# Expert biases and parameters gathered from one table, only where a stream's expert changes

## Chip, cores and metric

The kernel runs on one core of a Trainium2 chip. The time is the device time of one launch in microseconds (us); the number given for a kernel is the median of its runs. The profile is of one further execution.

## What is computed

The program is one layer of a graph network, a linear-attention mixer beside it, and a mixture of experts on their sum. The change touches the mixture of experts alone. It has 1250 rows of width D = 512, 16 experts, the best two experts for a row, and a hidden width I = 384 (so the first product makes 768 columns, gate and up interleaved):

```python
def swiglu5(h, alpha, gate_scale, up_shift, gate_clamp_raw, up_clamp_raw):
    gate_clamp = jax.nn.softplus(gate_clamp_raw)
    up_clamp = jax.nn.softplus(up_clamp_raw)
    g = jnp.clip(h[..., ::2], -gate_clamp, gate_clamp)
    u = jnp.clip(h[..., 1::2], -up_clamp, up_clamp)
    return g * jax.nn.sigmoid(g * alpha) * gate_scale * (u + up_shift)
...
gate_probs = jax.nn.softmax(xf @ gate_w + gate_b, -1)
w, idx = jax.lax.top_k(gate_probs, 2)
w = w / jnp.sum(w, axis=-1, keepdims=True)
he = jnp.einsum('nd,edh->enh', xf, expert_w1) + expert_b1[:, None, :]
te = swiglu5(he, a[:, 0], a[:, 1], a[:, 2], a[:, 3], a[:, 4])   # a = expert_act, five numbers an expert
oe = jnp.einsum('enh,ehd->end', te, expert_w2) + expert_b2[:, None, :]
y = jnp.einsum('ne,end->nd', cw, oe)                            # cw: the two weights of each row
return y + z                                                    # z: the same with a shared expert
```

## The kernel before

`moe` (from line 2285) is a program with semaphores written out by hand for five engines. It sorts the 2500 (row, expert) pairs into tiles of 64 rows with one expert each (HALF = 64). There are room and indices for 54 tiles. They are laid out as six streams of nine tiles (STREAMS = 6, TURNS = 9), and a stream is a run of consecutive tiles with a weight buffer of its own (`ew1[s]`, `ew2[s]`). Two streams work side by side: stream 2k on partitions ("lanes") 0 to 63, stream 2k+1 on lanes 64 to 127. So the loop has 27 steps, PAIRS = 27. Step i works on side `i % 3`, that is streams 2(i % 3) and 2(i % 3)+1, at turn `i // 3`. The bias ring has three buffers too (U = 3), so buffer `i % U` belongs to side `i % 3`.

For the inputs of the reference the experts get 71, 5, 1044, 7, 450, 335, 0, 2, 12, 2, 1, 13, 245, 0, 313 and 0 rows, which is 49 filled tiles. Along the streams the expert of the next turn is another one after step 2, 3, 5, 6, 7 and 8 in the even stream alone, after steps 4 and 11 in both, after step 22 in the odd and after step 23 in the even one: 12 changes in the 48 stream turns.

Routing first: POOL scatters the rows into their slots in DRAM with indirect DMAs (line 2478, ten for each of the two choices), while PE computes the shared expert. Then, for each step i:

- PE transposes the slot rows (line 2805), forms the first product (`up_pe`, line 2820, in two pieces of columns), transposes the gated rows (line 2868) and forms the second product (line 2883). The first piece of step i+1 stands ahead of the transposes of step i, its second piece ahead of the second product of step i. The first piece of step i waits for `next_w1_in` of both its streams.
- DVE adds the biases to the first product (`glu_dve`, line 2918, reads `eb1[u]`), clips (2922, 2923) and multiplies (2925, 2928). ACT takes the sigmoid (2944) with the expert's factor. All take their scalars from `eprm[u]`.
- ACT scales the result with the row's weight (line 2963), POOL scatters it to DRAM (line 2993).
- POOL gathers the weights for the next turn of both streams with one indirect DMA for each stream and matrix (`next_weights`, line 2972): those of w1 once `up_mm` of step i is there, those of w2 once `down_mm` is. The index table `weights_of` has an index beyond the bound for every lane but lane 0 where the expert stays the same, so those rows are skipped. A w1 row is 12,288 bytes in a lane, a w2 row 6,144.
- SP's `load_bias(i + 3)` loads the biases of the step three further on as soon as the buffer is free (`glu_made`): for each of the two streams it reads the expert's number from `slot_expert` into a register, then issues one DMA that spreads the expert's 768 biases over 64 lanes (line 2755, 192 KB) and one that spreads its eight parameters (line 2757, 2 KB, from `param_dram`). `load_slots` loads the slot rows, ten steps ahead.

POOL's indirect DMAs run on the software queue (q0 in the profile), SP's on a hardware queue (q1). Both use the same 16 DMA engines. All helper DMAs of SP carry line 114, so they are told apart by their tiles: `m_eb`, `m_eprm`, `rows`.

Of the kernel before, what the change touches and what calls it, by code (L numbers as in the profile page):

```python
# [16 lines left out]
ds = bass.ds  # L17
# [2267 lines left out]
def moe(c, x, w_all, cols_mem, cols, rows, slot_dram, back_dram, out):  # L2285
# [17 lines left out]
    param_dram = nc.dram_tensor("swiglu_params", [EXPERTS + 1, 8], F32)  # L2303
# [16 lines left out]
    first_w2_in = [c.sem(f"e_first_w2_in{s}") for s in range(STREAMS)]  # L2320
    next_w1_in = [c.sem(f"e_next_w1_in{s}") for s in range(STREAMS)]
    next_w2_in = [c.sem(f"e_next_w2_in{s}") for s in range(STREAMS)]
    weights_of_made = c.sem("r_weights_of_made")
# [9 lines left out]
    with ExitStack() as ctx:  # L2333
# [4 lines left out]
        eb1 = ring("m_eb1_", [128, 2 * FFN_I])  # L2338
        eprm = ring("m_eprm", [128, 8])
# [78 lines left out]
        rounds = lambda tile: tile // U + 1  # L2418
# [6 lines left out]
        def route_sp():  # L2425
            sp = c.sp
            load(sp, prm[0:EXPERTS, 0:5], a["L0_ffn_expert_act"]).then_inc(prm_in, 16)
            load(sp, prm[EXPERTS:EXPERTS + 1, 0:5], a["L0_ffn_shared_act"].rearrange("(a n) -> a n", a=1)).then_inc(
                prm_in, 16)
            load(sp, shared_b2[:], a["L0_ffn_shared_b2"].partition_broadcast(P)).then_inc(b2_in, 16)  # L2430
            for n in range(2):
                load(sp, b1[:, n, :], a["L0_ffn_shared_b1"].rearrange("(c p n) -> p n c", p=128, n=2)[:, n, :]).then_inc(
                    b1_in, 16)
            for q in range(SIDE):
                load(sp, b2[q * SQUARE:q * SQUARE + EXPERTS, :], a["L0_ffn_expert_b2"]).then_inc(w2_in, 16)
            load(sp, w2, chunks(a["L0_ffn_shared_w2"])).then_inc(w2_in, 16)
            sp.wait_ge(prm_made, 2)
            load(sp, param_dram[:, :], prm[:]).then_inc(prm_passed, 16)
            sp.wait_ge(prm_passed, 16)
            load(sp, shared_prm[:], param_dram[EXPERTS, :].partition_broadcast(128)).then_inc(prm_passed, 16)  # L2440
# [129 lines left out]
        def slots_dve():  # L2570
# [173 lines left out]
        def load_bias(i):  # L2744
            sp = c.sp
            u = i % U
            if i >= U:
                sp.wait_ge(glu_made, i - U + 1)
            for e, s in enumerate(streams(i)):
                j = tile_of(s, turn(i))  # L2750
# [24 lines left out]
        def experts_sp():  # L2775
# [4 lines left out]
            for i in range(U):  # L2780
                load_bias(i)
# [127 lines left out]
        def glu_dve(i):  # L2909
# [4 lines left out]
            v.wait_ge(bias_in[u], 64 * rounds(i))  # L2914
# [3 lines left out]
            v.tensor_tensor(by_half(h[u]), by_unit(psum[0:128, at:at + 2 * FFN_I]), by_unit(eb1[u][:]), ALU.add).then_inc(  # L2918
# [18 lines left out]
        def sigmoid(i):  # L2937
            s = c.act
            u = i % U
            s.wait_ge(bias_in[u], 64 * rounds(i))  # L2940
# [24 lines left out]
        def experts_pool():  # L2965
# [11 lines left out]
            g.wait_ge(weights_of_made, 1)  # L2977
            for i in range(PAIRS):
# [115 lines left out]
```

## Time and profile before

| | |
|---|---|
| median of 3 runs | 2438.06 us (2435.76 to 2438.35) |
| the profiled execution | 2439.28 us |
| its span, first to last instruction | 2437.3 us |
| mean granted TensorE clock | 0.993 |
| last first-piece matmuls (step 26) start | 2398.94 us |
| expert loop | about 2144 to 2407 us of the span |

The page gives PE busy for 97% of the span. The parts to read are those of the expert loop: the windows of it (busy time of each engine, the granted clock, the share of the 16 DMA engines' time in use, GB/s), the idle time of PE ahead of an instruction and what released it, the DMA queues by window, and POOL's own order of time.

### The profile page before, as it was taken

The page shows a single profiled execution, that of the slowest core. Times are in us where ns is not written, and L with a number is a line of the kernel's source. Part 1 is how long each engine was busy: PE and PEld are TensorE (multiplying, and loading weights), DVE is VectorE, ACT ScalarE, POOL GpSimd, SP SyncE. Part 2 cuts the span into 40 slices and gives each one's busy share as a digit, 9 for nine tenths or more (in the row PEclk, how much of TensorE's full clock was granted, in tenths as well). Part 3 has the DMA queues.
Part 4 walks back from the last instruction along what each step waited for, and adds up shares of the span by engine and source line. Part 5 has one row for each costly group of instructions (what it writes and reads, how often), then busy time and mean ns, then how long its engine had stood idle before and what let it go on. Part 6 is the DMA issues. An engine that isn't in the chain of part 4 may idle for free. (4 is left out here: it accounts for less than half of the span.)

```text
span 2437.3 us, 27998 instructions
## 1 busy us (share of the span) xinstructions
PE 2368.2 (97%) x9345; PEld 1402.0 (58%) x9345; DVE 1413.3 (58%) x2941; ACT 962.6 (39%) x1663; POOL 896.7 (37%) x1247
## 2 busy tenths in 40 slices
PE   8999999999999999999999999999999999988998
PEld 4565655545676556577556567666567664533443
DVE  7897671432776653677654477655377565633345
ACT  5885643221665211466221266321166422212221
POOL 2005202030565430365341165351065534434564
PEclk9999999999999999999999999999999999999999
DMA  5401101330566310366210266410066611679637
GB/s 166 138 18 32 44 13 52 93 102 18 134 156 156 124 57 18 90 152 156 80 42 22 57 159 156 124 42 22 18 150 161 165 41 48 219 251 322 215 89 235
DMA packets 138367, 264.31 MB, mean 108 GB/s; under 512 B 53038, under 2 KB 54814, under 8 KB 135884
## 3 DMA queue, kind: packets, MB, share of 16 engines
q1 hardware_dynamic: 93214, 159.89, 22.7%
q0 software_dynamic: 43664, 100.31, 15.4%
q10 hardware_dynamic: 1346, 2.33, 0.3%
q8 instruction: 76, 1.25, 0.2%
q14 instruction: 67, 0.55, 0.1%
HBM read 212.90 MB, written 31.93 MB: 100 GB/s over the span
## 5 line engine op out<-in xcount | busy, mean ns | idle before, releaser
L114 POOL DMA_DIRECT2D cols<-w x720 | 353.7, 499 | 592.7 <-DVE w L808 576.9
L691 PE MATMUL psum<-cols,rows 128*128 128x256 f32 (+1 forms) x1600 | 371.1, 380 | 7.2 <-DMA cols<-w 7.2
L677 PE MATMUL psum<-g_k_cols,g_q_cols 128*125 128x512 f32 (+1 forms) x960 | 362.0, 514 | 2.5 <-DVE g_row_max L794 2.5
L871 ACT ACTIVATE g_prob<-g_prob,g_row_max 125x1250 f32<-125x1250 f32 x160 | 214.0, 1338 | 307.9 <-DVE g_row_max L794 306.2
L691 PEld LDWEIGHTS psum<-cols,rows 128*128 128x128 f32 (+1 forms) x1600 | 303.8, 190 | 47.5 <-DMA cols<-w 8.6
L794 DVE CUSTOM_DVE_ANT_0 g_prob<-psum,ln_count 125x1250 f32<-125x1250 f32 x160 | 233.6, 1460 | 142.8 <-PE psum L677 142.8
L677 PEld LDWEIGHTS psum<-g_k_cols,g_q_cols 128*125 128x125 f32 x960 | 179.8, 188 | 173.2 <-issue 161.5
L808 DVE STREAM_TRANSPOSE w<-g_prob 128x1280 f32<-128x1280 f32 x160 | 241.2, 1508 | 11.2 <-ACT g_prob L877 11.2
L877 ACT ACTIVATE g_prob<-g_prob,g_row_max 125x1250 f32<-125x1250 f32 x160 | 214.1, 1338 | 58.3 <-DVE g_row_max L784 58.3
L2820 PE MATMUL psum<-m_ew,m_x_cols 128*64 128x256 f32 (+1 forms) x576 | 155.0, 499 | 16.9 <-DMA cols<-in_L_ffn_expert_w,m_weights_of 7.5
L704 PE MATMUL psum<-g_wo,g_q_cols 128*125 128x512 f32 x320 | 143.7, 593 | 1.8 <-ACT g_q_cols L883 1.8
L747 PE MATMUL psum<-w,g_k_cols 128*125 128x512 f32 x320 | 143.6, 592 | 0.0
L661 PE MATMUL psum<-w,cols 128*128 128x512 f32 (+1 forms) x320 | 139.3, 592 | 0.0
L2918 DVE TENSOR_TENSOR m_work<-psum,m_eb 128x768 f32<-128x768 f32 x27 | 40.9, 1514 | 150.3 <-PE psum L2820 129.8
L379 PE MATMUL psum<-cols,w 128*128 128x375 f32 (+1 forms) x416 | 115.3, 426 | 0.0
L661 PEld LDWEIGHTS psum<-w,cols 128*128 128x128 f32 (+1 forms) x320 | 60.0, 187 | 71.7 <-issue 71.5
L379 PE MATMUL psum<-rows,w 128*128 128x375 f32 (+1 forms) x368 | 101.2, 426 | 0.0
L2820 PEld LDWEIGHTS psum<-m_ew,m_x_cols 128*64 128x64 f32 x576 | 58.8, 139 | 72.9 <-issue 64.6
L333 POOL TENSOR_TENSOR rows<-cols 128x750 f32<-128x750 f32 (+1 forms) x16 | 20.7, 1293 | 211.6 <-ACT cols L515 211.6
L2972 POOL DMA_INDIRECT m_ew<-in_L_ffn_expert_w,m_weights_of x64 | 64.9, 1015 | 87.6 <-PE psum L2883 58.4
L1667 DVE TENSOR_SCALAR p_shared<-iota,p_edge_sum 125x250 f16<-125x250 f16 x334 | 95.3, 286 | 0.0
L429 DVE TENSOR_TENSOR g_k_cols<-g_k_cols,psum 128x375 f32<-128x375 f32 (+1 forms) x32 | 15.4, 481 | 136.6 <-PE psum L379 136.6
(392 smaller groups left out, 3936.5 us busy)
## 6 DMA issues: line engine op xcount, KB each, us to landing
cols<-w POOLq DMA_DIRECT2D x720, 80.0 KB, 3.3
cols<-w SPq DMA_DIRECT2D x560, 80.0 KB
m_eb<-in_L_ffn_expert_b SPq DMA_DIRECT2D x54, 192.0 KB
w<-in_L_gnn_m_w SPq DMA_DIRECT2D x8, 1024.0 KB
slot_rows<-p_kf SPq DMA_DIRECT2D x1, 7128.0 KB, 32.7
rows<-slot_rows SPq DMA_DIRECT2D x54, 132.0 KB, 5.2
m_ew<-in_L_ffn_expert_w SPq DMA_DIRECT2D x4, 1536.0 KB, 14.5
slot_outputs<-slot_rows SPq DMA_DIRECT2D x1, 5000.0 KB
```

What stands on the lines that cost most here:

```text
L114: return eng.dma_start(out, in_, allow_slow_non_contiguous=True)
L379: ins = pe.matmul(c.bank(SEVEN_BANKS[p][u], width), left, right, start=(k == 0 and p in (1, 5, 6, 7)), stop=(k == 1), skip_group_check=True)
L661: ins = pe.matmul(c.bank(V_BANKS[t], D, r), y_cols[:, k, t * 128:t * 128 + r], w[2][:, k, :], start=(k == 0), stop=(k == KC - 1))
L677: ins = pe.matmul(psum[0:P, at:at + width], q_cols[:, h, t * P:(t + 1) * P], k_cols[:, h, start:start + width], start=True, stop=True)
L691: ins = pe.matmul(c.bank(6 + g % 2, 256).rearrange("p (u a i) -> p u a i", u=2, a=SIDE), rows[0:r, j, h * 128:(h + 1) * 128], turned_keys[ ...
L704: ins = pe.matmul(c.bank(t % 2, D, P), q_cols[:, k, t * P:(t + 1) * P], wo[:, k, :], start=(k == 0), stop=(k == KC - 1))
L747: ins = pe.matmul(c.bank(t % 2, D, P), k_cols[:, k, t * P:(t + 1) * P], w[2][:, k, :], start=(k == 0), stop=(k == KC - 1))
L794: v.tensor_tensor_reduce(prob[0:P, u, 0:N], psum[0:P, at:at + N], ln_count[:, t, :], -SCORE_SCALE, -NOT_AN_EDGE / 10, ALU.add, ALU.min, ro ...
L808: v.transpose(square[s][:, :, u, :].rearrange("p b (j i) -> p b j i", i=SQUARE), prob_squares[u]).then_inc(squared, 1)
L871: s.activation(prob[0:P, u, 0:N], prob[0:P, u, 0:N], ACT.Exp, bias=row_max[:, u, 0:1], scale=-1.0, accum_out=row_max[:, u, 2:3]).then_inc( ...
L877: s.activation(prob[0:P, u, 0:N], prob[0:P, u, 0:N], ACT.Identity, scale=row_max[:, u, 3:4]).then_inc(prob_made, 1)
L2820: ins = pe.matmul(psum[lanes(e), at:at + cn], x_cols[u][:, k, lanes(e)], ew1[s][:, k, c0:c0 + cn], start=(k == 0), stop=(k == KC - 1))
```

## The change

One DRAM table, `unit_params`, gets a row of 776 numbers for each expert: 768 biases and 8 parameters. SP fills it during routing with two DMAs. The first three steps' buffers are loaded from it by SP as before, with one DMA for each stream instead of two. All later ones are gathered by POOL with one indirect DMA for each step (128 lanes, index table `bias_of`) into the side's buffer, between the gathers of w1 and of w2, after a wait for `glu_made`. `bias_of` skips as `weights_of` does: where a stream's expert stays, its lanes (but lane 0) are skipped and the buffer keeps what it has. DVE makes `bias_of` with three more small operations behind `weights_of`. `eprm` is now a view of the last eight columns of `eb1`.

```diff
@@ routing
             sp.wait_ge(prm_made, 2)
-            load(sp, param_dram[:, :], prm[:]).then_inc(prm_passed, 16)
+            load(sp, unit_dram[:, 0:2 * FFN_I], a["L0_ffn_expert_b1"]).then_inc(units_passed, 16)
+            load(sp, unit_dram[:, 2 * FFN_I:UNIT_ROW], prm[0:EXPERTS]).then_inc(units_passed, 16)
+            load(sp, param_dram[:, :], prm[EXPERTS:EXPERTS + 1]).then_inc(prm_passed, 16)
             sp.wait_ge(prm_passed, 16)
-            load(sp, shared_prm[:], param_dram[EXPERTS, :].partition_broadcast(128)).then_inc(prm_passed, 16)
+            load(sp, shared_prm[:], param_dram[0, :].partition_broadcast(128)).then_inc(prm_passed, 16)
...
             v.tensor_copy(weights_of[:], weights_f[:]).then_inc(weights_of_made, 1)
+            v.scalar_tensor_tensor(expert_f[:, 1:], same[:, 1:], lane_of[:, 1:2], expert_f[:, 1:], ALU.mult,
+                                   ALU.add).then_inc(step, 1)
+            n += 1
+            v.wait_ge(step, n)
+            for e in range(2):
+                v.tensor_copy(bias_of[lanes(e)].rearrange("p (q s) -> p q s", s=SIDES),
+                              expert_f[lanes(e)].rearrange("p (s e q) -> p e q s", e=2, q=TURNS)[:, e]).then_inc(
+                                  weights_of_made, 1)
@@ SP
-        def load_bias(i):
+        def load_first_bias(i):
...
-                load(sp, eb1[u][lanes(e), :], a["L0_ffn_expert_b1"][ds(of, 1), :].rearrange(
-                    "l o -> (l o)").partition_broadcast(HALF)).then_inc(bias_in[u], 16)
-                load(sp, eprm[u][lanes(e), :], param_dram[ds(of, 1), :].rearrange(
-                    "l o -> (l o)").partition_broadcast(HALF)).then_inc(bias_in[u], 16)
+                load(sp, eb1[i][lanes(e), :], unit_dram[ds(of, 1), :].rearrange("l o -> (l o)").partition_broadcast(
+                    HALF)).then_inc(bias_in[i], 16)
...
             for i in range(PAIRS):
-                if i + U < PAIRS:
-                    load_bias(i + U)
                 if i + R < PAIRS:
                     load_slots(i + R)
@@ DVE and ACT
-            v.wait_ge(bias_in[u], 64 * rounds(i))
+            v.wait_ge(*((next_bias_in[u], 16 * turn(i)) if turn(i) else (bias_in[u], 32)))
...
@@ POOL
                     next_weights(i, ew1, w1_rows, next_w1_in)
+                    g.wait_ge(glu_made, i + 1)
+                    g.indirect_dma_start(
+                        out=eb1[side(i)][:], out_offset=None, in_=unit_dram[:, :],
+                        in_offset=bass.IndirectOffsetOnAxis(ap=bias_of[:, i + SIDES:i + SIDES + 1], axis=0),
+                        bounds_check=EXPERTS - 1, oob_is_err=False).then_inc(next_bias_in[side(i)], 16)
                     g.wait_ge(down_mm, i + 1)
                     next_weights(i, ew2, w2_rows, next_w2_in)
```

## Rows read from the trace of the kernel before

**Rows 1.** The page's first part: busy us, share of the span, instructions.
```profile
PE 2368.2 (97%) x9345; PEld 1402.0 (58%) x9345; DVE 1413.3 (58%) x2941; ACT 962.6 (39%) x1663; POOL 896.7 (37%) x1247
```
**Rows 2.** Windows: stretch, its us, engines' busy us, PE clock, DMA share, GB/s.
```profile
2084.00:2090.00 6.00, 6.00 (x16) 2.77 (x15) 5.39 (x18) 1.85 (x3) 3.96 (x5) 1.00 0.96 390
...
2189.00:2264.00 75.00, 62.19 (x343) 26.81 (x341) 25.29 (x35) 15.48 (x28) 36.94 (x48) 0.95 1.02 317
2280.00:2302.00 22.00, 20.16 (x116) 8.39 (x114) 10.10 (x14) 5.58 (x10) 12.98 (x17) 1.00 0.91 304
2302.00:2400.00 98.00, 98.00 (x567) 42.53 (x569) 44.48 (x79) 24.36 (x45) 58.42 (x75) 1.00 0.43 134
```
**Rows 3.** Chain that ended last: start us, us, what; steps 2 and 5, a wait.
```profile
2167.88 3.65 PE psum L2820 x16
...
2194.50 3.43 PE psum L2820 x16
2197.93 0.48 PE psum L2868 x3
2198.41 0.44 PE psum L2805 x4
2198.84 1.88 PE psum L2820 x16
2200.72 2.60 PE psum L2883 x12
...
2249.80 14.39 DMA m_ew<-in_L_ffn_expert_w,m_weights_of
```
**Rows 4.** PE in order of time: start, us, ..., [idle before it, releaser].
```profile
2204.90 3.65 PE L2820 MATMUL psum<-m_ew,m_x_cols 128*64 128x512 f32 x16 [1.60 <-DMA m_ew<-in_L_ffn_expert_w,m_weights_of]
2220.01 1.08 PE L2820 MATMUL psum<-m_ew,m_x_cols 128*64 128x512 f32 x1 [6.09 <-DMA cols<-in_L_ffn_expert_w,m_weights_of]
2233.97 0.61 PE L2820 MATMUL psum<-w,m_x_cols 128*64 128x512 f32 x1 [2.15 <-DMA m_ew<-in_L_ffn_expert_w,m_weights_of]
2253.52 0.61 PE L2820 MATMUL psum<-m_ew,m_x_cols 128*64 128x512 f32 x1 [1.39 <-DMA cols<-in_L_ffn_expert_w,m_weights_of]
2264.44 0.61 PE L2820 MATMUL psum<-w,m_x_cols 128*64 128x512 f32 x1 [1.90 <-DMA m_ew<-in_L_ffn_expert_w,m_weights_of]
2301.92 3.65 PE L2820 MATMUL psum<-m_ew,m_x_cols 128*64 128x512 f32 x16 [1.10 <-DMA m_ew<-in_L_ffn_expert_w,m_weights_of]
```
**Rows 5.** DMA queues (packets, MB, share of 16 engines) and issues, 2189 to 2264.
```profile
q0 software_dynamic: 4371, 19.13, 80.0%
q1 hardware_dynamic: 3263, 4.55, 21.7%
...
m_eb<-in_L_ffn_expert_b SPq DMA_DIRECT2D x13, 192.0 KB
```
**Rows 6.** The same view, 2280 to 2302.
```profile
q1 hardware_dynamic: 1077, 1.41, 22.3%
...
m_eb<-in_L_ffn_expert_b SPq DMA_DIRECT2D x4, 192.0 KB
```
**Rows 7.** The same view, 2345 to 2380: on q1 nothing but bias loads.
```profile
q1 hardware_dynamic: 1299, 1.59, 14.8%
...
m_eb<-in_L_ffn_expert_b SPq DMA_DIRECT2D x8, 192.0 KB
```
**Rows 8.** POOL in order of time: last gather of w1, first of w2.
```profile
2201.31 1.00 POOL L2972 DMA_INDIRECT cols<-in_L_ffn_expert_w,m_weights_of  x1 [0.30 <-issue]
2204.10 0.99 POOL L2972 DMA_INDIRECT m_ew<-in_L_ffn_expert_w,m_weights_of  x1 [1.79 <-PE psum L2883]
```
**Rows 9.** SP's queue in order of time: the load of the shared parameters.
```profile
2066.46 0.35 SPq L114 DMA_DIRECT2D m_shared_prm<-swiglu_params  x1
```
**Rows 10.** DVE in order of time: `weights_of` made, first use of the shared parameters.
```profile
2085.93 0.19 DVE L2635 CAST m_weights_of<-m_x_cols 128x54 uint32<-128x54 f32 x1
...
2086.87 0.98 DVE L2701 TENSOR_SCALAR m_work<-m_work,m_shared_prm 128x500 f32<-128x500 f32 x2
```

More of the change, by code:

```diff
@@ L2302, in moe @@
     RANK, TOTAL, LOGIT, TURN, OUT = 6, 7, 5, 6, 7
-    param_dram = nc.dram_tensor("swiglu_params", [EXPERTS + 1, 8], F32)
+    UNIT_ROW = 2 * FFN_I + 8
+    param_dram = nc.dram_tensor("shared_params", [1, 8], F32)
+    unit_dram = nc.dram_tensor("unit_params", [EXPERTS, UNIT_ROW], F32)
     prm_in, b2_in, w2_in, b1_in, prm_passed = c.sems(
@@ L2320, in moe @@
     first_w2_in = [c.sem(f"e_first_w2_in{s}") for s in range(STREAMS)]
+    next_bias_in = [c.sem(f"e_next_bias_in{u}") for u in range(U)]
     next_w1_in = [c.sem(f"e_next_w1_in{s}") for s in range(STREAMS)]
     next_w2_in = [c.sem(f"e_next_w2_in{s}") for s in range(STREAMS)]
-    weights_of_made = c.sem("r_weights_of_made")
+    weights_of_made, units_passed = c.sems("r_weights_of_made", "r_units_passed")
     stored = [c.sem(f"e_stored{u}") for u in range(U)]
@@ L2337, in moe @@
         hidden = ew[3][:, 0:IC * N].rearrange("p (c n) -> p c n", c=IC)
-        eb1 = ring("m_eb1_", [128, 2 * FFN_I])
-        eprm = ring("m_eprm", [128, 8])
+        eb1 = ring("m_eb1_", [128, UNIT_ROW])
+        eprm = [v[:, 2 * FFN_I:UNIT_ROW] for v in eb1]
+        bias_of = sb("m_bias_of", [128, PAIRS], U32)
         x_all = sb("m_x_cols", [128, U, KC, 128])
@@ L2417, in moe @@
         flat = lambda v: v.rearrange("p t e -> p (t e)")
-        rounds = lambda tile: tile // U + 1
         GROUPS = [(start, width, k) for start, width in SPANS for k in range(IC)]
@@ L2740, in shared_down_dve @@
                 v.tensor_tensor(x[:, t, :], x[:, t, :], c.bank(s_bank(t), D, P), ALU.add).then_inc(s_added, 1)
-        def load_bias(i):
+        def load_first_bias(i):
             sp = c.sp
-            u = i % U
-            if i >= U:
-                sp.wait_ge(glu_made, i - U + 1)
             for e, s in enumerate(streams(i)):
-                j = tile_of(s, turn(i))
+                j = tile_of(s, 0)
                 of = sp.value_load(slot_expert[0:1, j:j + 1], min_val=0, max_val=EXPERTS - 1)
-                load(sp, eb1[u][lanes(e), :], a["L0_ffn_expert_b1"][ds(of, 1), :].rearrange(
-                    "l o -> (l o)").partition_broadcast(HALF)).then_inc(bias_in[u], 16)
-                load(sp, eprm[u][lanes(e), :], param_dram[ds(of, 1), :].rearrange(
-                    "l o -> (l o)").partition_broadcast(HALF)).then_inc(bias_in[u], 16)
+                load(sp, eb1[i][lanes(e), :], unit_dram[ds(of, 1), :].rearrange("l o -> (l o)").partition_broadcast(
+                    HALF)).then_inc(bias_in[i], 16)
         def load_first_weights(s):
@@ L2779, in experts_sp @@
                 load_first_weights(s)
-            for i in range(U):
-                load_bias(i)
+            sp.wait_ge(units_passed, 32)
+            for i in range(SIDES):
+                load_first_bias(i)
             sp.wait_ge(scattered, 16 * 2 * NT)
@@ L2917, in glu_dve @@
             at = 2 * (i % 2) * BANK
-            v.tensor_tensor(by_half(h[u]), by_unit(psum[0:128, at:at + 2 * FFN_I]), by_unit(eb1[u][:]), ALU.add).then_inc(
+            v.tensor_tensor(by_half(h[u]), by_unit(psum[0:128, at:at + 2 * FFN_I]), by_unit(eb1[u][:, 0:2 * FFN_I]), ALU.add).then_inc(
                 e_biased, 1)
@@ L2939, in sigmoid @@
             u = i % U
-            s.wait_ge(bias_in[u], 64 * rounds(i))
+            s.wait_ge(*((next_bias_in[u], 16 * turn(i)) if turn(i) else (bias_in[u], 32)))
             s.wait_ge(e_clipped, 2 * i + 1)
@@ L2975, in next_weights @@
                         bounds_check=EXPERTS * 128 - 1, oob_is_err=False).then_inc(ready[s], 16)
-            g.wait_ge(weights_of_made, 1)
+            g.wait_ge(weights_of_made, 3)
             for i in range(PAIRS):
```

## The prediction

> **What bounds the kernel now.** I read the page's first part, then the windows of the expert loop, then PE's idle time in them. PE is busy 97% of the span [rows 1], so work taken from another engine is worth only what PE waits for it. From 2302 to 2400 us PE is busy 98.00 of 98.00 us [rows 2]: nothing taken from SP, POOL or the DMA engines can shorten that stretch. One undisturbed step is 3.43 + 0.48 + 0.44 + 1.88 + 2.60 = 8.8 us of PE [rows 3]. From 2189 to 2264 it is otherwise: PE is busy 62.19 of 75 us while the 16 DMA engines are in use all the time (1.02), and from 2280 to 2302 PE is busy 20.16 of 22 us with the DMA engines at 0.91 [rows 2]. Each idle time of PE there ends with a gathered w1: 1.60, 6.09, 2.15, 1.39 and 1.90 us in the first burst, 1.10 in the second [rows 4]. These bursts are steps 2 to 8 and step 11, where experts change and whole weight rows must be moved.
>
> The first burst is a backlog. The gather that ends the wait at 2264.44 was issued at 2249.80 and took 14.39 us [rows 3], and the ones before it queued likewise. So the time of step 11's first matmuls is set by the DMA work queued ahead of its w1, not by PE and not by single waits. The granted clock shows the same. After the wait of 6.09 us a matmul takes 1.08 us where it takes 0.61 after a shorter one [rows 4], and the clock of the burst is 0.95 [rows 2]. If that loss went away, PE would only wait longer for the next w1, since those land when the DMA engines are through. I count nothing for it.
>
> **The change part by part.** (1) Removed on SP's queue: 48 bias loads and 48 parameter loads in the loop. SP itself is not on the chain here; its issues cost nothing and save nothing. What counts is the DMA engines' time. In the stretch 2345 to 2380 q1 carries bias loads alone, four steps of them: 14.8% of 35 us is 5.2 us, so 1.30 us of all 16 engines for a step with 0.40 MB [rows 7]. In the burst q1 takes 21.7% of 75 us, 16.3 us, for 4.55 MB, that is 3.6 us a MB [rows 5]. Thirteen loads of 192 KB and their parameters are 6.5 to 6.75 steps, 2.66 MB, so 9.5 us (8.7 by the quiet price).
>
> (2) Added on POOL's queue: 24 gathers. Only changed streams move rows: 64 lanes of 3,104 bytes, 0.20 MB each. Ahead of the w1 that ends the burst (gathered in step 8) stand those of steps 2 to 7, with seven changes: 448 rows, 1.39 MB, at the same 3.6 us a MB 5.0 us. Lanes that are skipped write a small packet each. I set these against the parameter packets that go.
>
> (3) What the first burst gives back. If the work is shared by all 16 engines evenly: 9.5 - 5.0 = 4.5 us. That is the upper end. The lower end comes from the diff. Of the seven changes six are in even streams, on lanes 0 to 63, one in each of the steps 2 to 7. Before, those lanes got 6.75 x 64 = 432 rows in this stretch, after it they get 6 x 64 = 384. If each DMA engine serves fixed lanes, the ones of the lower half keep 384/432 of their bias work and save 9.5 x 48/432 = 1.1 us, while the others save nearly all of theirs, which is no use: a gather has landed when its last part has. No row names the engine of a packet. I take 1.9 us, nearer to the lower end, because a wait goes by the last part and not by the mean; what is above 1.1 stands for engines that run faster when their neighbours have less to do.
>
> (4) The second burst. q1 takes 22.3% of 22 us, 4.9 us for 1.41 MB, 3.5 us a MB; its four bias loads with what is left of the ones before are about 0.87 MB, 3.0 us [rows 6]. After, only step 11 gathers, both streams, 0.40 MB, 1.4 us. The saving is 1.6 us on all lanes, since both halves change. PE idles 22 - 20.16 = 1.84 us there [rows 2], of which 1.10 is the wait at 2301.92 [rows 4], with the w1 of step 12 behind everything. The saving ends that wait; of the 0.7 us before it little, as fewer bias loads stand ahead of that one. I take 1.2 (0 to 1.8). What is late next is PE itself, as from 2302 on.
>
> (5) POOL. A gather is 1.0 us and 0.3 us ahead of it; between the last w1 gather (ends 2202.31) and the first of w2 POOL idles 1.79 us, waiting for the second product [rows 8]. The new wait for `glu_made` is for DVE's last step of the same side's values, which must be over before the transposes that precede that product, so it is through earlier. 1.3 us fits into 1.79. Cost nothing; if the cover were gone (a step in which the gathers start late), the w2 gathers, the scatter and the next w1 gathers queued behind would be later by up to 1.3 us, and those who wait are PE for w1 and DVE for the scatter's buffer. Outside the bursts a w1 gather is issued some 10 us before its use, inside them the queue is long anyway. Bound: 0 to +1.3 us, taken 0.
>
> (6) The bias now waits on the software queue, behind its w1. The first matmuls of a step start when w1 is in and end 3.43 + 0.48 + 0.44 + 1.88 = 6.2 us later [rows 3]; only then DVE needs the bias. A step's bias is at most 128 rows, 1.4 us by the price above. Margin 4.8 us, cost nothing.
>
> (7) Routing. SP issues two more DMAs before the shared parameters, 0.35 us each plus gaps, and DVE gets three operations of about 0.2 us [rows 9, 10]. The shared parameters were issued at 2066.46 and are first used by DVE at 2086.87 [rows 9, 10], 20 us later; ACT's first use of them is a wait only. DVE's 0.6 us delay the shared expert's first values, while PE works through (6.00 of 6 us from 2084 to 2090) [rows 2] with groups in hand. Six first bias DMAs instead of twelve: the same bytes. Taken 0, from -0.3 to +0.6.
>
> Sum: -1.9 - 1.2 = -3.1 us (from -6.4 to +1). The profiled execution's 2439.28 us becomes 2436.2; it lies 1.2 above the median of the runs, so against the median 2438.06 - 3.1 = 2435.0.
>
> The one rule that speaks on term (3): the Trainium skill, page "DMA: Bandwidth & Descriptors", section "The descriptor swizzle", says that a transfer over 128 partitions is split by partition, lanes 0 to 63 on engines 0 to 7 and lanes 64 to 127 on engines 8 to 15. By it term (3) is 1.1 and the whole -2.3, 2435.8 us. No row here shows the engine of a packet, so the range keeps both ends.
>
> **The rivals.** *Even sharing.* The 16 engines are pulled along by one shared limit, so bytes count wherever they go: 4.5 + 1.6 = 6.1 us, 2432.0. For it speaks that the DMA share is 1.02 on the mean of all engines, with none seen idle [rows 2]. Against it that this mean says nothing of which engine is last.
>
> *No gain.* The skipping does not work for the biases, or the saved part lands on engines that were never last. Then the burst carries about what it did; 2438, within 1 us.
>
> *Slower: the software queue is the bound by itself.* q0 took 80.0% and q1 21.7% of the burst [rows 5]. If q0's rings run at their own pace and q1's share was filled into gaps, taking the loads off q1 gives nothing back, and 448 rows come on top in the queue that PE waits for. Price: q0 needed 0.80 x 75 = 60 us for 19.13 MB, 3.1 us a MB; 1.39 MB is +4.4 us in the first burst and 0.40 MB +1.3 in the second: 2443.8. It decides if the gathers of w1 land later than before relative to their issue, while q1 is nearly empty. Against it: the shares add up to the whole, and what one queue takes the other lacks. The Trainium skill, page "DMA: Bandwidth & Descriptors", section "SWDGE vs HWDGE vs iDMA", sends plain loads to SP's hardware path and calls the software path the one for irregular transfers; a gather that skips is one, so I give the rule no more than this rival's chance.
>
> **How the numbers follow.** Forecast (-1 to -4.8 us): 0.50. Even sharing or better (-4.9 and beyond): 0.28. No gain: 0.12. Slower: 0.10, nearly all of it by over 0.2%. A measurement of this kernel can tell about 0.2%, 4.9 us, from no change, that is the bounds 2433.2 and 2442.9. Even sharing lies just beyond the lower one, the forecast and no gain lie between. So faster 0.28, same 0.61, slower 0.11. The range leaves out the far part of even sharing and most of the slower case: 2430.0 to 2441.5.
>
> **What the profile after would show.** No `m_eb` or `m_eprm` issue of SP after routing, and 24 more indirect DMAs of about 1 us on POOL. In the burst q1's share falls from 21.7% to about 9% (slot rows only), and q0's MB rise by about 1.4. The waits of PE stay, the last one of the first burst ending 1 to 2.5 us earlier after step 5's start than the 69.94 us from 2194.50 to 2264.44. The wait of 1.10 us of the second burst is gone or nearly so. From there every step is 8.8 us. It is wrong if DVE's line 2918 waits for a DMA of the biases (term 6), if the chain runs through POOL outside the bursts (term 5), if the first matmuls of step 2 come later than 2167.88 [rows 3] (term 7), or if the burst shortens by 4 us or more (term 3 mis-sized, even sharing).

## The result, and the profile after

The changed kernel takes 2424.53 us (median of 6, 2422.26 to 2426.42) against 2438.20 for the kernel before (6 runs, 2435.76 to 2439.85): ratio 0.9943, 95% interval 0.9932 to 0.9954, 13.7 us faster. The forecast was 2435.0 with a range down to 2430.0, so it was wrong: the sign was right, the size less than a quarter of what was measured. The profiled execution takes 2425.6 us, 13.7 less than the one before.

The first thing to look for is where on the way the 13.7 us come in. I cut the expert loop at the starts of first-piece matmuls: step 0 to 2, 5 to 11 (the first burst), 11 to 15 (the second), 15 to 26. Windows of the kernel before, cut so (columns as in [rows 2]):

```profile
2144.42:2167.88 23.46, 16.71 (x84) 6.72 (x84) 6.27 (x9) 2.88 (x6) 2.23 (x2) 0.85 0.93 348
2194.33:2264.44 70.11, 56.86 (x308) 24.02 (x305) 23.02 (x33) 14.22 (x26) 33.84 (x43) 0.95 1.02 317
2264.44:2301.92 37.48, 35.64 (x205) 15.51 (x205) 13.90 (x19) 8.74 (x16) 21.25 (x28) 1.00 0.74 236
2301.92:2398.77 96.85, 96.85 (x561) 42.18 (x563) 43.71 (x77) 23.49 (x44) 58.50 (x75) 1.00 0.44 136
```

The same windows of the changed kernel:

```profile
2142.53:2166.95 24.42, 17.16 (x83) 6.81 (x84) 6.11 (x8) 2.44 (x5) 3.23 (x3) 0.79 0.93 344
2193.40:2252.83 59.43, 53.86 (x309) 23.26 (x305) 22.01 (x32) 13.86 (x26) 39.62 (x49) 1.00 0.99 354
2252.83:2288.42 35.59, 35.47 (x204) 15.59 (x206) 14.23 (x20) 8.26 (x16) 25.78 (x32) 1.00 0.60 211
2288.42:2385.22 96.80, 96.80 (x563) 41.97 (x561) 44.29 (x78) 24.34 (x45) 69.47 (x86) 1.00 0.31 99
```

The first burst is 10.68 us shorter, the second 1.89, the quiet rest 0.05; 0.93 was there before step 2. PE alone needs six steps of 8.8 us for the first burst, 52.8. Its idle time there falls from 13.25 to 5.57 us, and its busy time by 3.0: the mean granted clock of the stretch was 0.95 and is now 1.00, so hardly a matmul runs at the lower of its two levels (1.2 GHz) any more. PE's waits for a w1 in this stretch, to be held against [rows 4] (in order of time, columns as there):

```profile
2213.36 0.61 PE L2827 MATMUL psum<-m_ew,m_x_cols 128*64 128x512 f32 x1 [2.19 <-DMA cols<-in_L_ffn_expert_w,m_weights_of]
2223.91 0.61 PE L2827 MATMUL psum<-w,m_x_cols 128*64 128x512 f32 x1 [1.53 <-DMA m_ew<-in_L_ffn_expert_w,m_weights_of]
2233.65 3.65 PE L2827 MATMUL psum<-m_ew,m_x_cols 128*64 128x512 f32 x16 [0.71 <-DMA m_ew<-in_L_ffn_expert_w,m_weights_of]
2243.38 0.61 PE L2827 MATMUL psum<-m_ew,m_x_cols 128*64 128x512 f32 x1 [0.71 <-DMA cols<-in_L_ffn_expert_w,m_weights_of]
2252.83 0.61 PE L2827 MATMUL psum<-w,m_x_cols 128*64 128x512 f32 x1 [0.43 <-DMA m_ew<-in_L_ffn_expert_w,m_weights_of]
```

The wait of 6.09 us is 2.19, and the matmul behind it takes 0.61 us, not 1.08. The weights wait for the DMA engines in both kernels (share 1.02 and 0.99), so look at what the engines move: 70.11 us at 317 GB/s are 22.2 MB before, 59.43 us at 354 GB/s are 21.0 MB after. Fewer bytes would explain a burst 5% shorter; it is 15% shorter. **The rate rose, and that is the part the forecast did not have.** The queues in this window, before:

```profile
q0 software_dynamic: 4060, 18.08, 80.6%
q1 hardware_dynamic: 2973, 4.08, 20.8%
```

and after, with two kinds of gather, how many of each were issued and their median time from issue to landing:

```profile
q0 software_dynamic: 4649, 19.33, 88.5%
q1 hardware_dynamic: 960, 1.62, 10.4%
...
m_ew<-in_L_ffn_expert_w,m_weights_of POOLq DMA_INDIRECT x16, 12.7
m_eb<-unit_params,m_bias_of POOLq DMA_INDIRECT x7, 12.8
```

The other steps of the forecast, in the changed kernel. POOL in order of time, to be held against [rows 8]:

```profile
2200.38 1.00 POOL L2979 DMA_INDIRECT cols<-in_L_ffn_expert_w,m_weights_of  x1 [0.30 <-issue]
2201.68 1.07 POOL L2995 DMA_INDIRECT m_eb<-unit_params,m_bias_of  x1 [0.30 <-issue]
2203.18 0.99 POOL L2979 DMA_INDIRECT m_ew<-in_L_ffn_expert_w,m_weights_of  x1 [0.42 <-issue]
```

The gather of 1.07 us stands in the idle time that was 1.79 and is 0.42. What DVE's bias add waits for, 2190 to 2300:

```profile
L2925 DVE TENSOR_TENSOR m_work<-psum,m_eb x12: 1508/1515/1522, 2191.0 to 2294.9; 128x768 f32<-128x768 f32 x12
its engine sat idle before it (us, times) until:
  PE psum L2827: 63.9, 12
```

All twelve times for the first product, never for the bias; the same view of the whole loop has 27 of 27. SP and DVE around the shared parameters, to be held against [rows 9, 10]:

```profile
2065.65 0.34 SPq L114 DMA_DIRECT2D m_shared_prm<-shared_params  x1
```
```profile
2084.44 0.39 DVE L2646 CAST m_bias_of<-m_x_cols 64x27 uint32<-64x27 f32 x2
...
2085.78 1.15 DVE L2714 TENSOR_SCALAR m_work<-m_work,m_shared_prm 128x500 f32<-128x500 f32 x2
```

### The profile page after: what moved, and what is told of

Same layout as the page of the kernel before. It is cut to its first block and busy times, and to the rows that moved or that the text cites. A ratio compares the mean times of both kernels' runs of the same rounds, so it can differ in the third digit from the quotient of the medians.

```text
span 2423.6 us, 27601 instructions
## 1 busy us (share of the span) xinstructions
PE 2364.5 (98%) x9345; PEld 1401.8 (58%) x9345; DVE 1413.8 (58%) x2944; ACT 962.8 (40%) x1663; POOL 921.8 (38%) x1271
## 5 line engine op out<-in xcount | busy, mean ns | idle before, releaser
L333 POOL TENSOR_TENSOR rows<-cols 128x750 f32<-128x750 f32 (+1 forms) x16 | 20.7, 1293 | 212.6 <-ACT cols L515 212.6
L704 PEld LDWEIGHTS psum<-g_wo,g_q_cols 128*125 128x125 f32 x320 | 57.7, 187 | 64.1 <-issue 60.0
```

Source lines behind the costliest of these rows:

```text
L704: ins = pe.matmul(c.bank(t % 2, D, P), q_cols[:, k, t * P:(t + 1) * P], wo[:, k, :], start=(k == 0), stop=(k == KC - 1))
```

## The experiments

Every kernel below the second line was timed in five rounds beside the kernel before on the same chip. The medians, the ratio to before (with its 95% interval), and the first burst (step 5 to 11) by the windows of the trace:

| kernel | biases and what else differs | us | ratio, 95% | first burst us | its GB/s |
|---|---|---|---|---|---|
| before | 2 broadcasts over 64 lanes, all steps | 2438.2 | | 70.11 | 317 |
| changed | gather over 128 lanes, skipping | 2424.5 | 0.9943 [0.9932, 0.9954] | 59.43 | 354 |
| after_again | the same | 2423.8 | 0.9949 [0.9934, 0.9964] | 59.38 | 353 |
| a_table_sp | table, SP, all steps | 2437.8 | 1.0002 [0.9992, 1.0012] | 69.18 | 325 |
| a_again | the same | 2436.8 | 0.9997 [0.9988, 1.0006] | 67.44 | 331 |
| c_skip_sp | table, SP, changed streams only | 2426.1 | 0.9961 [0.9947, 0.9974] | 61.91 | 340 |
| b_gather_all | gather, all rows | 2428.7 | 0.9964 [0.9953, 0.9975] | 60.15 | 372 |
| e_no_loads | none after step 2 | 2420.9 | 0.9940 [0.9926, 0.9953] | 55.63 | 351 |
| h_sp_behind_w1 | a, issued when w1 has landed | 2430.4 | 0.9975 [0.9964, 0.9985] | 66.16 | 329 |
| h_again | the same | 2433.1 | 0.9981 [0.9969, 0.9993] | 65.67 | 331 |
| g_odd_all | gather, odd lanes never skipped | 2423.8 | 0.9950 [0.9932, 0.9967] | 60.06 | 372 |
| m_spare_sp | changed + 2 unused loads, 64 lanes | 2443.8 | 1.0022 [1.0010, 1.0034] | 75.46 | 317 |
| l_spare_half | the same, half the columns | 2432.6 | 0.9976 [0.9967, 0.9986] | 68.55 | 329 |
| j_pool_plain | a's loads on POOL's queue | 2439.1 | 1.0003 [0.9993, 1.0014] | 69.32 | 328 |
| p_one_dma | a, one load over 128 lanes | 2424.2 | 0.9936 [0.9920, 0.9951] | 61.69 | 361 |
| n_spare_wide | changed + 1 unused load, 128 lanes | 2432.1 | 0.9973 [0.9962, 0.9984] | 67.73 | 352 |
| o_spare_mixed | m, every other lane | 2431.2 | 0.9978 [0.9967, 0.9989] | 67.52 | 354 |
| d_own_rows | before, reads 64 different rows | 2436.5 | 0.9996 [0.9983, 1.0010] | 68.42 | 326 |
| i_slots_late | changed, slot rows held back | 2416.3 | 0.9918 [0.9901, 0.9935] | 54.12 | 361 |
| k_slots_late | before, slot rows held back | 2428.2 | 0.9955 [0.9940, 0.9970] | 59.28 | 346 |

The median is the measure of a kernel; the burst is one execution each, but three kernels profiled twice give it within 0.05, 1.7 and 0.5 us. The time ahead of step 2 moves more than that from one execution to the next (step 2 starts at 2166.95 in one profile of the changed kernel and at 2164.24 in the other), so differences there are not read.

**First four: which half of the change does it.** a_table_sp is the changed kernel with its gather taken out and SP's loads put back, from the new table:

```diff
+                if i + U < PAIRS:
+                    load_first_bias(i + U)
...
-                    g.wait_ge(glu_made, i + 1)
-                    g.indirect_dma_start(
...
```

> The kernel after with its table, but SP loads both streams' rows of it on its own queue for every step, as before (one DMA of 3,104-byte rows instead of two DMAs), and POOL gathers no biases. Theory M (bytes and the queue they are on decide): nothing is saved in the bursts, the time is that of the kernel before, 2437 to 2438. Theory N (the number of DMAs and the small 32-byte packets were the cost): the small packets are gone, so most of the gain of 13.7 us is here, 2430 or less.

2437.8 us: the merged tables, and half as many DMAs and small packets, give nothing. c_skip_sp issues those loads only for streams that change (`for e in CHANGED.get(i - U, ())`):

> As the run with SP's loads from the table, but SP loads only those streams' rows whose expert changes; which they are is written into the program for these inputs. Theory BYTES (the DMA work that is left out is the whole gain, whichever queue it was on): same as the kernel after, 2424.5 within 1.5. Theory QUEUE (packets of SP's queue mixed among the gathered weight rows slow these, so moving them to POOL's queue is part of the gain): about half of the rows of the bursts still come on SP's queue, so about half of the gain, near 2431.

b_gather_all is the changed kernel without the operation that makes `bias_of` skip:

```diff
-            v.scalar_tensor_tensor(expert_f[:, 1:], same[:, 1:], lane_of[:, 1:2], expert_f[:, 1:], ALU.mult,
-                                   ALU.add).then_inc(step, 1)
```

> The kernel after without the skipping: each of the 24 gathers moves all 128 lanes' rows, so the bytes are those of the kernel before, on POOL's queue. Theory BYTES: 0.20 MB more in each of 6 steps of the first burst and two whole steps of 0.40 MB in which nothing changes, near the kernel before, 2435 to 2438. Theory QUEUE: the gain stays but for the added rows at their own price of 3.6 us a MB, about +5 on the kernel after, near 2430.

e_no_loads has SP's loop load nothing at all (`LOADED = lambda i: (0, 1) if i < U else ()`):

> As the run with SP's loads from the table, but after the first three steps no biases or parameters are loaded at all (the later experts' biases and parameters are left out, those of the first steps stand in for them). This is the ceiling. By the price of my prediction (3.6 us a MB of bias rows) the kernel before less 9.5 + 3.0 us, 2426, and so above the kernel after, which can't be; by the measured gain the seven changes that the kernel after still gathers cost at least their own bytes, so 2418 to 2422.

From a, skipping alone gives 11.7 us (c), gathering alone 9.1 (b), both 13.3, no traffic at all 16.9. They do not add up, so either one takes away much of the same expensive thing. Neither BYTES nor QUEUE held for both kernels: c came where BYTES put it, and b, 9 us below a with the same bytes, where QUEUE did. The sharpest pair is a and b, since they move the same bytes. Their windows, a first:

```profile
2192.62:2261.80 69.18, 57.16 (x309) 24.22 (x305) 21.82 (x32) 13.68 (x26) 32.76 (x42) 0.93 1.01 325
```
```profile
2195.21:2255.36 60.15, 55.48 (x308) 23.73 (x305) 22.05 (x32) 13.91 (x26) 39.51 (x49) 0.97 1.01 372
```

69.18 x 325 and 60.15 x 372 are 22.5 and 22.4 MB. DMA share 1.01 in both, and yet one is 9 us faster. So the same full share stands over two rates.

**Place in the queue, or the queue itself?** h_sp_behind_w1 keeps a's loads but gives them b's place (SP's later slot-row loads stand behind the same wait):

```diff
+            if i >= U:
+                for s in streams(i):
+                    sp.wait_ge(next_w1_in[s], 16 * turn(i))
```

> The table read by SP in every step, as a_table_sp, but SP waits for the gathered w1 of the same step before it issues that step's two bias loads. So the bias bytes stand behind the same weights as in b_gather_all (2428.66 us), while they still travel on q1. Two theories explain why b_gather_all is 9 us faster than a_table_sp with the same bytes. ORDER: on q1 a bias load is served at once, ahead of all weight rows that POOL has queued; on the software queue it takes its turn behind w1. Then this kernel gives what b_gather_all gives, 2427 to 2430 us, and the first burst (step 5 to step 11, first-piece matmuls) lasts 60 to 62 us. MIX: packets of q1 among q0's weight rows make those rows take longer, wherever they stand. Then it stays near a_table_sp, 2435 to 2438 us, the burst 67 to 69 us. Loads that come when the next w1 is in flight cost the same there. I give ORDER 0.35, MIX 0.45, and 0.2 to something between.

> a_table_sp once more, on one chip with the next kernel: its median against h_sp_behind_w1's was 7.4 us, while in the two profiles the stretch from step 5 to 15 differed by 4.1 us. Expected 2437 to 2438 us.

> h_sp_behind_w1 once more, on one chip with a_again, for the share of ORDER. If ORDER is most of the 9 us: 2430 us and at least 6 us below a_again in the burst. If it is the smaller part: 2433 to 2435 us, and 3 to 4 us below in the burst, with 325 GB/s there as in a_table_sp.

By the medians of the second pair the place is worth 3.7 us of the 9 (7.4 in the first), by the bursts 3.0 and 1.8. The rate does not move (325 and 331 for a, 329 and 331 for h). So the place is a part, its size not better known than 2 to 7 us, and the rate is something else. m_spare_sp shows the cost from the other side, by adding it to the changed kernel:

```diff
+                if i + U < PAIRS:
+                    sp.wait_ge(glu_made, i + 1)
...
+                    for e in range(2):
+                        load(sp, spare[lanes(e), :], unit_dram[0:1, :].rearrange("l o -> (l o)").partition_broadcast(HALF))
```

> The changed kernel, with SP's two bias-sized loads in each step put back on top (each spreads row 0 of the table over 64 lanes of a buffer that nobody reads, as soon as the step's values are made). The gathers stay. If the loads on q1 are what cost the 13.7 us, all of it comes back: 2437 to 2440 us, the first burst 68 to 72 us (59.4 in the changed kernel). If the gain came from the merging of the two DMAs or from the waits of SP and DVE for the biases, which are not put back, it stays below 2428 us.

+19.3 us, more than the whole gain and more than expected (2440 at most): it came back without the merged DMAs, and on top of the gathers. So what cost was there to be had is in those loads. l_spare_half takes columns `0:FFN_I + 4` of each row:

> m_spare_sp (the changed kernel with two unused bias-sized loads of SP in each step, 2443.8 us against 2424.5, so +19.3) with half the columns: as many packets on q1, each of 1,552 bytes for 3,104. If the cost goes by packets, nearly all of it stays: 2440 to 2443 us. If it goes by bytes, half of it does: 2433 to 2436 us. The packet's own duration on q1 shows the rest.

+8.0 us by the medians, 9.1 in the burst against 16.0. As many packets with half the bytes cost about half, so the cost goes by the bytes rather than by the number of packets. j_pool_plain issues a's loads from POOL, where the gather stood:

```diff
-                    g.indirect_dma_start(
...
+                    for e, s in enumerate(streams(i)):
...
+                        load(g, eb1[side(i)][lanes(e), :], unit_dram[ds(of, 1), :].rearrange("l o -> (l o)").partition_broadcast(HALF))
```

> The biases of every step are moved by two plain broadcast DMAs, the ones of a_table_sp word for word, but POOL issues them, at the place of the gather. They carry the same bytes as a_table_sp and b_gather_all, in 3,104-byte packets like the first; they stand on POOL's software queue like the second. MIX (what costs is the hardware queue's packets among the software queue's): as b_gather_all, 2427 to 2431 us, burst (step 5 to 11) 60 to 63 us, some 360 GB/s. SIZE (what costs is the number of packets: a gathered bias packet has 6,208 bytes, two lanes, and the trace has 53 to 55 packets over 1 KB in each us of the burst in every kernel so far): as a_table_sp, 2435 to 2439 us, burst 67 to 70 us. POOL's own time is larger by the second issue and two register loads; if the chain runs through POOL outside the burst, steps of over 8.8 us after 2302 us show it. MIX 0.5, SIZE 0.4.

2439.1 us. Its queues in the burst, and its bias loads:

```profile
q0 software_dynamic: 4929, 21.00, 92.3%
q1 hardware_dynamic: 968, 1.64, 9.2%
...
m_eb<-unit_params POOLq DMA_DIRECT2D x13, 194.0 KB, 15.1
```

q1 is as empty as in b, and it does not help. MIX, the theory I held to be likeliest, has fallen. SIZE had the time right, but not its reason: I had expected small packets, and these are large (the packet records give 6,208 bytes, as for the gather), with a burst of 69.3 us all the same. Left was what j and a have in common and b has not: each load writes 64 lanes, or each reads one row.

**Lanes or row?** p_one_dma writes 128 lanes with one load (`LOADED = lambda i: (0,)`, `load(sp, eb1[u][:, :], ... partition_broadcast(128))`), on SP's queue, as early as a:

> a_table_sp (2437.8 and 2436.8 us) with one broadcast DMA over 128 lanes in each step in the place of two over 64. It takes the expert of the even stream for both, so the odd stream's biases are another expert's in the steps where the two differ; nothing of the time hangs on values. Same bytes, same packets, same queue, same moment. j_pool_plain has ended the two theories on the queue and the packet's size: its loads were on the software queue in 6,208-byte packets like the gathered ones and it still took 2439.1 us. Two are left. HALF: a plain DMA over 64 lanes writes to only half of the lanes' ways into the buffers, yet all of its rows are on their way at once, so it runs slowly and holds back the weight rows; a gather over 128 lanes, and one plain DMA over 128, do not. Then this kernel is near b_gather_all, 2427 to 2431 us, burst 59 to 62 us. HOT: a broadcast reads one row of DRAM for all its lanes at a time, which is slow, and slower for 128 lanes from one row than for 64: 2436 to 2440 us. HALF 0.6, HOT 0.25.

Its window, its queues and its bias loads:

```profile
2190.92:2252.61 61.69, 55.16 (x309) 23.72 (x307) 21.74 (x31) 13.29 (x25) 33.10 (x42) 0.97 0.99 361
```
```profile
q0 software_dynamic: 3906, 18.21, 79.1%
q1 hardware_dynamic: 1821, 3.99, 19.1%
...
m_eb<-unit_params SPq DMA_DIRECT2D x6, 388.0 KB, 8.6
```

and a_table_sp's loads in its burst:

```profile
m_eb<-unit_params SPq DMA_DIRECT2D x12, 194.0 KB, 9.0
```

388 KB over 128 lanes land in 8.6 us, 194 KB over 64 lanes in 9.0. With all bias bytes still on SP's queue, and one row read 128 times, the kernel takes 2424.2 us, as fast as the change and 3 us below what HALF gave for it. n_spare_wide does the same to m (`load(sp, spare[:, :], ... partition_broadcast(128))`):

> m_spare_sp (the changed kernel with two unused loads over 64 lanes in each step: +19.3 us, burst 75.5 us for 59.4) with one unused load over 128 lanes in their place, the same bytes. HALF: it costs about what the gathered rows of every stream cost b_gather_all against e_no_loads, 4.6 us in the burst: 2428 to 2432 us, burst 63 to 66 us. HOT: as m_spare_sp, 2441 to 2446 us.

2432.1 us, and the burst 67.7 us, each just beyond the end of HALF's range and far from HOT's: +7.6 us where two loads over 64 lanes cost 19.3. d_own_rows reads different rows in the kernel before:

```diff
-                load(sp, eb1[u][lanes(e), :], a["L0_ffn_expert_b1"][ds(of, 1), :].rearrange("l o -> (l o)").partition_broadcast(HALF))
+                load(sp, eb1[u][lanes(e), :], a["L0_ffn_expert_w1"][ds(of, 1), 0:HALF, :].rearrange("l p o -> p (l o)"))
```

> The kernel before, but each bias DMA reads 64 different rows of 3,072 bytes (the first 64 of the expert's w1) in the place of one row 64 times. The biases are wrong by that, and nothing else is. HOT: the slow read goes away, 2427 to 2431 us. HALF: the lanes written are the same, so the time is that of before, 2437 to 2440 us.

2436.5 us, half a us from HALF's range and 5 from HOT's. The interval of its ratio holds 1: reading one row is not it. The last doubt was whether a load is dear for being in one half of the lanes, or for being small and one of two. o_spare_mixed is m with `spare[e:128:2, :]` for `spare[lanes(e), :]`:

> m_spare_sp (two unused loads of 64 lanes in each step on top of the changed kernel, +19.3 us) with other lanes: one load takes the even lanes 0, 2, ... 126, the other the odd ones, so each has 64 rows as before, but half of them in either half of the buffer. LANES (what is dear is that all 64 rows go into one half of the lanes): the cost is that of n_spare_wide, +7.6 us: 2430 to 2434 us, burst 65 to 69 us. COUNT (what is dear is a DMA of 64 rows, or two of them): the cost is that of m_spare_sp: 2441 to 2446 us, burst 74 to 77 us. LANES 0.75.

> The changed kernel once more, on one chip with the one above, as its base: 2423 to 2426 us, the first burst 58 to 61 us.

+7.3 us on one chip with its base, as for the wide load. The queues of q1 in the bursts of m, n and o, in this order:

```profile
q1 hardware_dynamic: 1995, 4.17, 19.9%
```
```profile
q1 hardware_dynamic: 1856, 4.08, 19.0%
```
```profile
q1 hardware_dynamic: 1978, 4.13, 19.5%
```

Nothing in these rows tells the three apart; the windows do, m first, then o:

```profile
2190.68:2266.14 75.46, 59.31 (x308) 24.77 (x305) 22.53 (x32) 14.19 (x26) 39.60 (x49) 0.91 0.99 317
```
```profile
2189.54:2257.06 67.52, 56.81 (x308) 23.89 (x305) 23.13 (x33) 14.22 (x26) 40.57 (x50) 0.95 0.99 354
```

So do the single packets of the gathered weights in the traces of the same windows. A packet of 12,288 bytes takes 559 ns on the mean in m, 509 in n, 504 in o and 508 in the changed kernel; one of 6,144 bytes 306, 277, 274 and 267. Loads that write all lanes leave the weight rows' packets as they are; loads that write one half make each of them longer. The kernel before has 584 and 328 ns. (j_pool_plain's 326 ns fit, its 516 for the large ones only in part.)

Against the 1.62 MB of the changed kernel, m puts 2.55 MB more on q1 for 16.0 us of burst, **6.3 us a MB; n 2.46 MB for 8.3, 3.4 us a MB; o 2.51 MB for 8.1, 3.2 us a MB.** A plain load that writes one half of the lanes costs about twice what it costs when it is spread over both.

For a gather this does not hold. Six of the seven gathers in the changed kernel's burst move rows to lanes 0 to 63 alone, and they cost 3.8 us over e_no_loads for 1.39 MB, 2.7 us a MB. In c_skip_sp plain loads of such rows cost 6.3 us for 1.21 MB, 5.2 us a MB. Their earlier place in the queue does not explain it: j_pool_plain's plain loads stood at the gather's place and cost 13.7 us over e_no_loads for 2.68 MB, 5.1 us a MB. Why a gather into one half is cheap and a plain load is not, no run here shows.

Why a plain load over one half is dear, no trace shows, since no record names an engine or a lane. The Trainium skill, page "SBUF — State Buffer", section "Door 1: The DMA port swizzle", gives a reason: the lanes 0 to 63 are reached over 8 of the 16 ports, and a transfer into 64 lanes is hardly faster than one into 32. Page "DMA: Bandwidth & Descriptors", section "Rules for kernel authors", asks for one 128-partition transfer in place of two halves. The first agrees with the measurements where the loads are plain, though no run here has a load over 32 lanes; the second agrees with a_table_sp against p_one_dma, 2437.8 for 2424.2 us. m against o tells which of them counts here: o still has two transfers of 64 rows, and it costs no more than n's one, so it is the lanes and not the number of transfers.

**Are a gather's rows tied to their lanes?** g_odd_all makes the skipping operation work on `[0:HALF]` alone:

> The changed kernel, but lanes 64 to 127 are never skipped: every step gathers 64 bias rows for the odd stream, changed or not. In steps 2 to 8 this adds six times 64 rows, 384 rows or 1.19 MB, all on the upper lanes, while w1 and w2 rows change there only in step 4. TIED (each DMA engine serves fixed lanes, the lower term of the forecast's step 3): the added rows go to engines that have little to do, the time is that of the changed kernel, 2424 to 2425.5 us. EVEN (all engines share the work): 1.19 MB at 3.1 to 3.6 us a MB are 3.7 to 4.3 us, capped by what b_gather_all lost against the changed kernel, 4.1 us: 2427.5 to 2428.7 us. I give TIED 0.5.

2423.8 us, the burst 60.06 for 59.43. Its window holds 60.06 x 372 = 22.3 MB, 1.3 more than the changed kernel's; 1.0 of that are bias rows (384 packets of 6,208 bytes for 224), at no cost that can be measured. At the 3.1 to 3.6 us a MB of EVEN 1.0 MB would be 3.1 to 3.6 us. Gathered rows on the upper lanes are all but free while the lower lanes have their six changes. The section "The descriptor swizzle" that the forecast weighed (the Trainium skill, page "DMA: Bandwidth & Descriptors") splits a transfer over 128 partitions into these two halves of lanes and of engines. It says nothing of a gather with skipped rows, but the measurement fits it. b_gather_all has the same burst, 60.15, since it moves the same bias rows there. Its median is 4.9 us above g's. In the two profiles the whole difference lies ahead of step 2 (2168.76 us for 2163.23), in the part that moves from one execution to the next; whether it belongs to the kernel is open.

**The other loads over 64 lanes.** The slot rows are such loads too. i_slots_late, in the changed kernel:

```diff
             for i in range(PAIRS):
+                if i == 2:
+                    sp.wait_ge(up_mm, 11)
                 if i + R < PAIRS:
                     load_slots(i + R)
```

> The changed kernel, but SP holds back the slot-row loads of steps 12 to 26 until the first product of step 10 is made, so q1 carries nothing of them while experts change in steps 2 to 8. Nothing is left out, only the order in time is another. If each packet of q1 costs the weight rows something, what was left on q1 (2.13 MB, 10.6% of 75 us = 8 us of all engines in the changed kernel) is still a cost: the first burst, 59.4 us in the changed kernel, comes nearer to the 52.8 us (six steps of 8.8 us) that PE needs by itself, 54 to 57 us, and the time is 2419 to 2422 us. The held-back loads (fourteen in a bunch, 1.9 MB) go out between 2248 and 2256 us, before the w1 rows of step 11 are wanted. If the gain of the change had nothing to do with q1's traffic as such (it came from the bias bytes' place or from their broadcast), the time stays at 2424 to 2425. If the bunch lands in front of the second burst's rows, it gives back up to 4 us there: step 11 to 15 longer than 37 us.

2416.3 us, 8.2 below the changed kernel, below the 2419 expected, and the fastest of all. First and second burst:

```profile
2189.10:2243.22 54.12, 53.02 (x309) 22.99 (x307) 21.74 (x31) 13.29 (x25) 39.01 (x49) 1.00 0.97 361
2243.22:2278.81 35.59, 35.42 (x206) 15.38 (x204) 14.48 (x21) 8.83 (x17) 26.53 (x33) 1.00 0.77 257
```

The first burst is 1.3 us above PE's own 52.8, and the held-back rows give nothing back in the second. k_slots_late does it to the kernel before (at step 9, `sp.wait_ge(up_mm, 11)`, then the loads of steps 12 to 18):

> The kernel before, with the slot-row loads of steps 12 to 18 held back as in i_slots_late, nothing left out. The slot rows are different rows of DRAM each, but every load of them is over 64 lanes. HALF: they cost what the bias loads cost by the MB, in m_spare_sp 16.1 us for 2.77 MB, 5.8 us a MB; fourteen loads of 135 KB are 1.9 MB, 11 us: the first burst (70.1) comes to 58 to 61 us, the time to 2427 to 2430 us. HOT: they are ordinary bytes at 3.1 us a MB or less, 6 us at most: 2432 us or more.

2428.2 us, the burst 10.8 us shorter. Its q1 carries 1.66 MB less than before's 4.08, so 6.5 us a MB: about the price of m, found on other loads in another kernel. Here the second burst pays 3.2 us back, 40.7 us for 37.5, since the bunch meets the bias loads there.

## Why the prediction was wrong

Term 3, the first burst, failed: 10.7 us measured for 1.9 forecast, and for 4.5 at its upper end. Two steps of the working made it so, the price in term 1 and the count by lanes in term 3. The terms that it is made of:

- **Term 1, the price of the removed loads, was mis-sized.** The forecast divided q1's share of time by its megabytes, 3.6 us a MB [rows 5]. That counts the time in which the loads' own packets are open. It leaves out what they do to the weight rows beside them. The kernel before against e_no_loads gives 14.5 us for 2.46 MB, 5.9 us a MB; m_spare_sp and k_slots_late give 6.3 and 6.5, the widest other pairs 4.7 (a_again against e_no_loads) and 7.4 (l_spare_half against the changed kernel). 3.6 was about right for loads spread over all lanes (2.6 in p_one_dma against e_no_loads, 3.4 and 3.2 in n and o). With the 6.3 of m_spare_sp, which does not rest on the burst that it is to explain, the removed 2.66 MB are worth 16.8 us, and less term 2 that leaves 11.8, against 10.7 measured. The burst can shorten by 17.3 at most, and as it nears that, each MB is worth less: i_slots_late takes 1.41 MB of half-lane loads off q1 and gains 5.3 us, 3.8 us a MB, where k_slots_late has 6.5.
- **Term 2, the added gathers, held.** Taken at 5.0 us; the changed kernel's burst is 3.8 us above that of e_no_loads, though near PE's limit.
- **The choice between the ends of term 3.** I was near the lower end because the lanes 0 to 63 keep 384 of 432 rows. The tie is borne out for gathered rows: g_odd_all's rows on the other lanes cost 0.6 us where even sharing asked for 3.1 or more. What was wrong is to count the removed loads in rows for a lane, as if a row cost the same in whichever DMA it came. By that count b_gather_all should have saved nothing; it saves 9 us. The rule of the Trainium skill that was weighed for it speaks of a transfer over 128 partitions, and the removed loads were over 64.
- **The clock.** I counted nothing for it. 3.0 of the 10.7 us are matmuls that run at the full clock again, 7.7 are idle time. Whether the clock's part would have turned into waiting, as I argued, no run separates. It is open.
- **Term 4** had 1.2, 1.89 was measured, just over the 1.8 that I had as its end: PE now fills 35.47 of 35.59 us there.
- **Terms 5, 6 and 7 held.** The gather fits between w1 and w2 with 0.42 us left, and every quiet step stays at 8.8 us. DVE never waits for a bias. The shared parameters are issued 0.8 us earlier than before and used 20 us later; step 2 is not late.
- **The sum's own ends**, -6.4 to +1, are by the ends of its terms -6.6 to +0.8. The measured -13.7 is outside either.
- **The signs to look for** told the miss: the burst shortened by more than 4 us, which the forecast had named as term 3 mis-sized. But they named even sharing as the cause, and g_odd_all speaks against that.

Of the rivals, *slower* is refuted in its mechanism: b_gather_all puts more on q0 than the changed kernel (20.7 MB for 19.3 in the burst) and is 9 us faster than the same bytes on q1. *Even sharing* had the direction and less than half of the size. The queue made no difference for these loads, the lanes did: p_one_dma sends all bias bytes through SP's queue and is as fast as the change. So the advice of the Trainium skill that was weighed there (page "DMA: Bandwidth & Descriptors", section "SWDGE vs HWDGE vs iDMA") neither helped nor hurt. The two rules of the Trainium skill cited above could have been a warning: every load that the change removes writes 64 lanes. They would not have given the whole case, since most of the gathers move rows of one half too.

A row that could have warned me was there, too: 317 GB/s at a share of 1.02 in the burst, 390 at 0.96 in the stretch from 2084 to 2090 [rows 2]. I read the share as the engines' limit and did not ask why a fuller share moved fewer bytes.

## What to carry to other kernels

Where a stretch is bound by the DMA engines, read bytes a second beside the share: a full share at a low rate can mean, as here, that some of the transfers are of a bad shape, and that taking those away gives more than their share of time. Look for plain loads that write one half of the lanes; spread them over all 128, or keep them out of the stretch in which weights are waited for. And price a removal by adding the same thing once more: unused loads like those of m_spare_sp, put on top of the kernel, price them at 6.3 us a MB, near the 5.9 that the removal gave, where the share of time said 3.6.

## What the runs showed that I had not expected

- The same bytes on q1 cost 6.3 us a MB when each plain load writes lanes 0 to 63 or 64 to 127, and 3.2 when each writes every other lane.
- Which queue carries them, and whether packets have 3,104 or 6,208 bytes, changed nothing that could be measured (2437.8 and 2436.8 against 2439.1 us).
- The half-lane loads lengthen the packets of the weight rows beside them: 559 ns for 508 in m_spare_sp (12,288 bytes).
- Gathered rows on lanes 64 to 127 were all but free while lanes 0 to 63 had as many: 1.0 MB for 0.6 us.
- Holding back loads that are needed much later, with one wait on SP, gave 8.2 us on top of the change, at no cost elsewhere.
